# Fusion block: embedded rows kept in a PSUM bank, token mix reading transposed tokens from PSUM, squares in the place of the columns, and another order of work

## The chip, the cores and the metric

One core of one Trainium2 chip. The metric is the device time of one execution in microseconds. The kernel before has a median of 1633.04 us in three runs.

## The reference, cut to what matters

64 pictures of 3x224x224 are cut into 196 patches of 768 numbers; each patch is normalised, multiplied by a 768x256 matrix and normalised again. 77 text tokens are put behind the 196 of the picture, 273 tokens in all. Then comes an attention block, whose attention, by the letters of its einsum, runs over the 16 heads of one token and not over tokens, and a feed-forward block with a token shift, each on normalised rows and added to its input.

```python
x = _layernorm(patches, ln1_g, ln1_b)
x = jnp.einsum('bnd,de->bne', x, W) + b
h = concatenate([_layernorm(x, ln2_g, ln2_b), txt], axis=1)
# attention on _layernorm(h); Q, K, V have the shape (n, heads, tokens, 16)
scores = jnp.einsum('nqhd,nkhd->nhqk', Q, K) * scale
o = jnp.einsum('nhql,nlhd->nqhd', softmax(scores), V).reshape(n, s, e)
h = h + (o @ Wo.T + bo)
# feed-forward on x = _layernorm(h):
x_prev = concatenate([zeros, x[:, :-1, :]], axis=1)
xr = mu_r * x + (1.0 - mu_r) * x_prev
xk = mu_k * x + (1.0 - mu_k) * x_prev
out = sigmoid(xr @ W_r.T) * (square(relu(xk @ W_k.T)) @ W_v.T)
h = h + out
```

## The kernel before, in words

Everything is float32; products are made from a high and a low part of each operand (three matmuls for one). Four pictures form a quad of 4 x 273 = 1092 tokens, cut into three chunks of 364 tokens. A chunk has three row tiles of 126, 126 and 112 rows. There are 16 quads, so 64 pictures and 48 chunks.

A picture passes through these jobs, in the names of the order: `load` (SP, L477: both halves into `xim`), `xcols` (ScalarE, L943: three copies into the column layout `xcols`), `x` (TensorE, L1106: transposes into PSUM), `xh` and `xl` (high and low part into `xT`, L951 on ScalarE, L770 on VectorE), `tok` (TensorE, L1118: two products with 98 patches each), `sq` (ScalarE, L955: squares), `ssq` (VectorE, L765: their sums), `stat`, `statc`, `statr` (sums over patches, L1125, L774, L780), `sqm`, `rstd1` (first scale), `yn` (VectorE, L786: scaled rows into `y`), `st2`, `mv2` (statistics of `y`, L790, L795), `rstd2`, `hg` (VectorE, L800: `y` less its mean times gain, in place), `h` (VectorE, L806: into `yh`), `hdma` (SP: rows into the chunk's tiles).

A chunk passes through: `st3` to `xnl` (normalisation, transpose, parts), `qkv` and `qb` (products and bias, L1026 and L843), `qkv_out`, `qk_in` (L514), `v_in` (through DRAM), `kspread` (ScalarE, L921), `qplace` (VectorE, L829), `s` (scores, L1075), `mx`, `sub`, `exp`, `pt`, `ptc` (L933), `av`, `rec`, `osb` (softmax and values; `osb` is VectorE's L758), `o_out` and `o_in` (through DRAM, nine pieces out and four in; `o_in` of the first two chunks of a quad waits for `o_out` of the chunk behind, one slot of 4000 steps later), `ont` (TensorE, L1152), `onh`, `onl` (L977, L849), `wo`, `h2`, `st4` to `rstd4`, `z`, `zt` (TensorE, L1166: transposed tokens in PSUM), `ztc` (ScalarE, L994: copied to `zT`), `d` (GpSimd, L654: difference of neighbours), `edge` (GpSimd, L660, L661), `mix` (VectorE, L872: four mixes of 128x364), `mixh`, `mixl`, `k`, `kr`, `ksq`, `kah`, `kal`, `r`, `rt`, `val`, `rv`, `add`, `out`.

The order of work is written out by hand in `AT`: each job has a step; a picture job comes again every 3000 steps, a chunk job every 4000, a quad takes 12,000. Every engine issues its jobs in the order of their steps and starts one when the semaphores that it waits for are up. The steps set an order and no times. SP issues all DMAs, in the same order.

`BANK` gives each product or transpose one of the eight PSUM banks. Before TensorE writes into a bank, `turn` makes it wait for the last reader (`READ`) of the job that had the bank before.

The rows that the mix uses are built as `dT` = token less its predecessor (for the first token of a picture the token itself), and `mix` = `dT` * mu + predecessor, where the predecessor is read from `zT` at one column less.

## Time and profile before

| | us |
|---|---|
| median of three runs | 1633.04 |
| lowest, highest | 1625.81, 1639.91 |
| the profiled execution | 1637.46 |
| its span | 1635.7 |

The span is the time from the first to the last instruction of the profiled execution. Busy time is the union of an engine's instructions; a wait is idle time of an engine just before an instruction, put down to what released it last. Matmuls overlap in the pipeline, so TensorE's busy time is not its time at peak. PE is TensorE, DVE VectorE, ACT ScalarE, POOL GpSimd, and SPq the DMA queue of SP.

### The profile page before, as it was taken

The numbers are of one execution on the slowest core, as the hardware profiler recorded it, in microseconds if no ns is written. First come the engines' busy times: TensorE is split into PE (matmuls) and PEld (weight loads), VectorE is DVE, ScalarE is ACT, GpSimd is POOL, SyncE is SP. The second block draws the span as 40 slices with busy tenths as digits, with TensorE's granted clock in tenths as the row PEclk, the third lists the DMA queues.
The fourth block names the chain that finished last, engine by engine and source line by source line (L and its number), as shares of the span: only waits on it lengthen the run. The fifth ranks groups of instructions, "written<-read, shape, count | busy, mean of one in ns | idle before, by whom it ended". The sixth has DMA issues, their size and how long they took to land. (4 is left out here: it accounts for less than half of the span.)

```text
span 1635.7 us, 53680 instructions
## 1 busy us (share of the span) xinstructions
PE 1454.6 (89%) x18762; PEld 1382.2 (85%) x18762; DVE 1332.3 (81%) x3075; ACT 1099.9 (67%) x2230; POOL 973.6 (60%) x1507
## 2 busy tenths in 40 slices
PE   4678899899999999999999999999999999998856
PEld 4677898898998898889898898998988988897756
DVE  5576888798988989898898888898898988888642
ACT  4455777677777776776777676777777776775543
POOL 2121566567656666666766765675675676576556
PEclk8798999999999999999999999999999999999988
DMA  4279979889877887888887896898898799887651
GB/s 121 59 141 138 141 147 150 125 159 157 143 157 141 147 155 143 150 137 165 149 140 157 151 141 127 167 157 141 152 154 140 151 159 140 156 151 118 131 74 37
DMA packets 702658, 227.65 MB, mean 139 GB/s; under 512 B 617470, under 2 KB 673854, under 8 KB 702394
## 3 DMA queue, kind: packets, MB, share of 16 engines
q1 hardware_dynamic: 702394, 224.23, 77.9%
q8 instruction: 153, 2.51, 0.8%
q14 instruction: 111, 0.91, 0.2%
HBM read 121.64 MB, written 89.64 MB: 129 GB/s over the span
## 5 line engine op out<-in xcount | busy, mean ns | idle before, releaser
L1026 PE MATMUL bank<-wqkv,xnT 128*126 128x384 f32 (+1 forms) x1728 | 354.2, 349 | 5.5 <-issue 5.5
L1118 PE MATMUL bank<-wtok,xT 128*98 128x258 f32 x2304 | 310.2, 290 | 12.0 <-DVE xT L770 11.4
L1026 PEld LDWEIGHTS bank<-wqkv,xnT 128*126 128x126 f32 (+1 forms) x1728 | 294.0, 185 | 18.3 <-issue 10.2
L1118 PEld LDWEIGHTS bank<-wtok,xT 128*98 128x98 f32 x2304 | 294.2, 171 | 14.6 <-DVE xT L770 13.2
L667 POOL TENSOR_TENSOR mixp<-mixf,mixp 128x364 fp32r<-128x364 f32 x192 | 185.2, 976 | 107.2 <-ACT mixp L1000 106.6
L921 ACT ACTIVATE arena<-qk,ymask 128x768 f32<-128x768 f32 x192 | 164.0, 926 | 97.6 <-DMA qk<-qkv_dram 97.6
L843 DVE TENSOR_TENSOR qkvt<-bank,bqkv 126x384 f32<-126x384 f32 (+1 forms) x288 | 154.0, 548 | 48.5 <-PE bank L1026 47.0
L654 POOL TENSOR_TENSOR dT<-zT 128x364 f32<-128x364 f32 x96 | 79.7, 851 | 153.9 <-ACT zT L994 153.9
L609 POOL TENSOR_TENSOR rs<-ve,small 126x3 f32<-126x3 f32 (+1 forms) x160 | 150.3, 940 | 12.5
L607 POOL TENSOR_TENSOR ve<-mv,small 126x3 f32<-126x3 f32 (+1 forms) x160 | 58.8, 368 | 158.8 <-DVE mv L865 104.0
L765 DVE TENSOR_REDUCE xs<-xim 84x14 f32<-84x1792 f32 x64 | 128.7, 2011 | 23.1 <-ACT xim L955 22.8
L872 DVE SCALAR_TENSOR_TENSOR mixf<-dT,mus,zT 128x364 f32<-128x364 f32 x192 | 125.8, 676 | 22.4 <-POOL zT L661 19.5
L943 ACT ACTIVATE xcols<-xim 84x640 f32<-84x640 f32 (+1 forms) x192 | 126.1, 693 | 25.4 <-DMA xim<-in_x 24.1
L1026 PE MATMUL bank<-woT,onT 128*126 128x256 f32 (+1 forms) x864 | 121.9, 287 | 12.4 <-DVE onT L849 12.1
L951 ACT ACTIVATE xT<-bank 128x420 fp32r<-128x420 f32 (+1 forms) x192 | 99.9, 532 | 44.5 <-PE bank L1106 44.2
L1026 PE MATMUL bank<-wrT,mixp 128*126 128x256 f32 (+1 forms) x864 | 124.9, 292 | 4.2 <-POOL mixp L667 3.7
L1026 PEld LDWEIGHTS bank<-woT,onT 128*126 128x126 f32 (+1 forms) x864 | 110.6, 186 | 17.7 <-DVE onT L849 16.9
L1026 PE MATMUL bank<-mixp,wkfT 128*128 128x364 f32 x576 | 123.5, 352 | 1.5 <-POOL mixp L667 1.4
L1075 PE MATMUL bank<-arena,qx 128*32 128x64 f32 x4608 | 83.0, 225 | 43.8 <-issue 43.8
L933 ACT ACTIVATE pt<-bank 64x384 f32<-64x384 f32 x192 | 93.0, 484 | 37.9 <-PE bank L1083 34.5
L682 POOL TENSOR_TENSOR h<-h,r 126x256 f32<-126x256 f32 x144 | 114.2, 807 | 6.1 <-DVE r L878 6.1
L1075 PEld LDWEIGHTS bank<-arena,qx 128*32 128x32 f32 x4608 | 74.1, 112 | 51.1 <-issue 47.4
(121 smaller groups left out, 3339.6 us busy)
## 6 DMA issues: line engine op xcount, KB each, us to landing
xim<-in_x SPq DMA_DIRECT2D x128, 294.0 KB
qk<-qkv_dram SPq DMA_DIRECT2D x48, 768.0 KB, 8.3
qkv_dram<-qkvt SPq DMA_DIRECT2D x96, 378.0 KB
arena<-qkv_dram SPq DMA_DIRECT2D x384, 48.0 KB, 3.9
qkv_dram<-qkvt SPq DMA_DIRECT2D x48, 336.0 KB
o_dram<-probs SPq DMA_DIRECT2D x288, 48.0 KB, 1.9
out<-h SPq DMA_DIRECT2D x96, 126.0 KB
on<-o_dram SPq DMA_DIRECT2D x64, 126.0 KB
```

The lines of the kernel that those rows point to most:

```text
L609: done.done(P.tensor_tensor(rs[:, :], ve[:, :], powt[0:part, 0:ve.shape[1]], ALU.pow))
L667: mix_lo.done(P.tensor_tensor(mixp[:, w, 1, kk, :], mixf[:, kk, :], mixp[:, w, 0, kk, :].bitcast(F32), ALU.subtract))
L682: out_sb.done(P.tensor_tensor(dst, dst, r[0:rows, i, :], ALU.add))
L765: x_stats.done(V.tensor_reduce(xs[:, :], xim[:, :].rearrange("p (w q) -> p w q", q=128), AX.X, ALU.add))
L843: qkv_sb.done(V.tensor_tensor(qkvt[0:rows, i, NQ * half:NQ * half + NQ], place("qkv", job)[0:rows, 0:NQ], bqkv[0:rows, :, :].rearrange("p ...
L872: mix_sb.done(V.scalar_tensor_tensor(out=mixf[:, kk, :], in0=dT[:, kk, :], scalar=mus[:, w, kk:kk + 1], in1=zT[:, kk, 0:CT], op0=ALU.mult, ...
L921: kb_sb.done(A.activation(kb[:, :, yy, :], qk[:, :, HD:2 * HD], ACT.Copy, scale=ymask[:, yy:yy + 1]))
L943: x_cols.done(A.activation(xcols[:, 128 * w0:128 * w1].rearrange("p (w r q) -> p w r q", r=HALF, q=PS), xim[:, :].rearrange("p (r w q) -> ...
L951: x_hi.done(A.activation(xT[:, 0, :, w0:w1], src, ACT.Copy))
L1026: ins = mm(psum, left(a, k), right(b, k), start=t == 0, stop=t == len(terms) - 1)
L1075: ins = mm(place("s", part)[32 * j:32 * j + 32, col:col + 64], qx[:, g, :, :].rearrange("p x q -> p (x q)"), kb[:, g, :, :].rearrange("p y ...
L1118: ins = mm(place("tok", c)[0:PT, 0:E + 2], xT[:, a, i0:i0 + GRID // 2, :].rearrange("p i w -> p (i w)"), wtok[:, b, ch, :], start=t == 0, ...
```

## The change

Four things. First, `y` is no tensor in SBUF any more but half a PSUM bank of its own (bank 7): `yn` writes it there, and `st2`, `hg` and `h` read it there; `yn` waits for that bank through `turn`, which VectorE may call now too. The masked statistics `sel`, which lay in `y`, get a small tensor. Second, `mix` reads the transposed tokens in their PSUM bank instead of `zT`. As that is the token itself and not its predecessor, `mus` holds mu - 1, and the memset of the predecessor at picture edges (L661) goes; a bank of `zt` is now given back by `mix` 2 or 3 and no longer by `ztc`. Third, the squares overwrite `xcols` instead of `xim`. So `load` waits for the three copies of the picture before instead of its reduce, `sq` waits for the transposes of its own picture, and the first copy of a picture waits for the reduce of the picture before. Fourth, all steps of `AT` and all banks are new: picture jobs have banks 3 and 1, chunk jobs 0, 2, 4, 5, 6.

```diff
-AT = dict(load=[0], xcols=[1345, 1388, 1607], sq=[2596], ssq=[2858], sqm=[3415, 4248], x=[1817, 2019, 2235],
-    xh=[1848, 2327, 2533], xl=[2074, 2593, 2661], tok=[2893, 3830], stat=[3940], statc=[4050], statr=[4305],
-    rstd1=[4411], txt=[8023], yn=[4758, 4836], st2=[4981, 5034], mv2=[5433, 5999], rstd2=[6371], hg=[6625, 6861],
-    h=[6868, 6960], hdma=[7063], st3=[10962, 11342, 11356], mv3=[11065, 11397, 11434], rstd3=[11873], xn=[12040,
-    12043, 12181], xt=[12258, 12294], xnh=[12466, 12535], xnl=[12759, 12786], hb=[16417], qkv=[13041, 13154, 13772,
-    14109, 14497, 14527], qb=[13342, 13376, 14009, 14120, 14637, 14838], qkv_out=[13386, 14854, 14929],
-    qk_in=[15678], v_in=[16977], qplace=[17149, 17224], kspread=[17070, 17106, 17203, 17246], s=[17531, 17701],
-    mx=[17623, 17710], sub=[17716, 17726], exp=[17794, 17831], pt=[17914, 17953], ptc=[18007, 18037, 18144, 18161],
-    av=[18175, 18232], rec=[18186, 18538], osb=[18451, 18546], o_out=[18883], o_in=[23572], ont=[24528, 24562],
-    onh=[24548, 24569], onl=[24813, 24817], wo=[24929, 25291, 25299], h2=[25035, 25379, 25541], st4=[25320, 25562,
...
+AT = dict(load=[0], xcols=[974, 1452, 2008], sq=[3314], ssq=[3606], sqm=[4006, 4551], x=[2368, 2528, 2871],
+    xh=[2472, 2955, 3124], xl=[2687, 3242, 3261], tok=[3423, 4348], stat=[3670], statc=[4035], statr=[4182],
+    rstd1=[4635], txt=[8796], yn=[5189, 5294], st2=[5527, 5530], mv2=[6117, 6421], rstd2=[7071], hg=[7159, 7405],
+    h=[7476, 7485], hdma=[8110], st3=[11601, 11697, 11879], mv3=[11949, 11981, 12005], rstd3=[12326], xn=[12347,
+    12371, 12403], xt=[12701, 12751], xnh=[12819, 12851], xnl=[13088, 13135], hb=[17111], qkv=[13369, 13634, 14369,
+    14664, 15014, 15279], qb=[13566, 14729, 14730, 14870, 15390, 15419], qkv_out=[15330, 15332, 15987],
+    qk_in=[16906], v_in=[17788], qplace=[17760, 17898], kspread=[17748, 17765, 17780, 17888], s=[18176, 18179],
+    mx=[18317, 18320], sub=[18371, 18448], exp=[18511, 18568], pt=[18545, 18617], ptc=[18591, 18662, 18778, 18835],
+    av=[18778, 18860], rec=[18886, 19014], osb=[18968, 19133], o_out=[19894], o_in=[24612], ont=[24927, 25140],
...
+BANK = dict(x=[3, 1, 3], tok=[3, 1], stat=[1], yn=[7], xt=[2, 6], qkv=[2, 6, 0, 4, 6, 4], s=[5, 4], pt=[5, 2],
+    av=[5, 0], ont=[4, 0], wo=[0, 5, 4], zt=[5, 0], k=[5, 2], r=[6, 2, 6], val=[2, 4, 6])
...
-        READ = dict(x=(x_lo, [1, 2, 3]), tok=(y_sb, [1, 2]), stat=(stat_sel, [1]), xt=(xn_lo, [1, 2]),
+        READ = dict(x=(x_lo, [1, 2, 3]), tok=(y_sb, [1, 2]), yn=(h_sb, [2]), stat=(stat_sel, [1]), xt=(xn_lo, [1, 2]),
-                    ont=(on_lo, [1, 2]), wo=(h2_sb, [1, 2, 3]), zt=(zT_sb, [1, 2]), k=(kr_sb, [1, 2]),
+                    ont=(on_lo, [1, 2]), wo=(h2_sb, [1, 2, 3]), zt=(mix_sb, [3, 4]), k=(kr_sb, [1, 2]),
...
-                            after(x_stats, q, k - 1, 1)
+                            after(x_cols, q, k - 1, 3)
...
+                            P.tensor_scalar(mus[:, :, :], mus[:, :, :], 1.0, None, ALU.subtract).then_inc(probs_clear, 1)
...
-                        edge_sb.done(P.memset(zT[:, :, b], 0.0))
...
-                        x_stats.done(V.tensor_reduce(xs[:, :], xim[:, :].rearrange("p (w q) -> p w q", q=128), AX.X, ALU.add))
+                        x_stats.done(V.tensor_reduce(xs[:, :], xcols[:, :].rearrange("p (w q) -> p w q", q=128), AX.X, ALU.add))
...
-                        h_sb.wait(dve, q, k - 1, 2)
+                        stat_sb.wait(dve, q, k - 1, 1)
...
+                    y = place("yn", 0)[0:PT, 0:2 * E].rearrange("p (c e) -> p c e", c=2)
...
-                            h_sb.wait(dve, q, k - 1, 2)
+                            if c == 0:
+                                turn(dve, q, s, "yn", 0)
...
-                                                               in1=zT[:, kk, 0:CT], op0=ALU.mult, op1=ALU.add))
+                                                               in1=place("zt", kk)[:, 0:CT], op0=ALU.mult, op1=ALU.add))
...
-                                x_tr.wait(act, q, k - 1, 3)
-                                x_sq.wait(act, q, k - 1, 1)
+                                x_stats.wait(act, q, k - 1, 1)
...
+                        x_tr.wait(act, q, k, 3)
                         x_cols.wait(act, q, k, 3)
-                        x_sq.done(A.activation(xim[:, :], xcols[:, :], ACT.Square))
+                        x_sq.done(A.activation(xcols[:, :], xcols[:, :], ACT.Square))
...
-                        mix_sb.wait(act, q, k - 1, 4)
+                        edge_sb.wait(act, q, k - 1, 1)
```

The steps that the text speaks of and that are cut above: `zt` was [26592, 26720] and is [27288, 27294]; `ztc` was [26852, 27151] and is [27372, 27410]; `mix` was [27723, 27748, 28355, 28501] and is [28082, 28139, 28650, 28666]; `mixl` was [28081, 28111, 29157, 30005] and is [28447, 28510, 29976, 30394]; `k` was [28326, 28668] and is [28866, 30101]; `out` was [32565, 33050, 33990] and is [33982, 34383, 35593].

## Rows read from the trace of the kernel before

**Rows 1.** The page: busy us of each engine, share of the span, instructions

```profile
PE 1454.6 (89%) x18762; PEld 1382.2 (85%) x18762; DVE 1332.3 (81%) x3075; ACT 1099.9 (67%) x2230; POOL 973.6 (60%) x1507
```

**Rows 2.** Stretches from:to, us: busy time of each engine, granted clock, DMA share, GB/s

```profile
100.00:1500.00 1400.00, 1298.23 (x17287) 1237.74 (x17286) 1210.23 (x2799) 990.93 (x2011) 867.38 (x1328) 0.99 0.84 147
300.00:1300.00 1000.00, 938.80 (x12434) 896.62 (x12437) 875.73 (x2021) 720.01 (x1469) 646.27 (x981) 0.99 0.84 148
1500.00:1636.00 136.00, 97.25 (x1110) 89.51 (x1108) 63.04 (x146) 65.25 (x141) 81.20 (x114) 0.89 0.50 84
```

**Rows 3.** Timeline of PE, transposes L1152: start, us, what, [idle before <-releaser]

```profile
688.95 0.85 PE L1152 MATMUL bank<-ident,on 126*128 126x126 f32 x6 [0.79 <-DMA on<-o_dram]
...
752.07 0.85 PE L1152 MATMUL bank<-ident,on 126*128 126x126 f32 x6 [1.46 <-DMA on<-o_dram]
...
783.12 0.85 PE L1152 MATMUL bank<-ident,on 126*128 126x126 f32 x6 [1.32 <-DMA on<-o_dram]
```

**Rows 4.** Waits of PE from 300 to 1300 us: total us, times, longest

```profile
PE bank L1075 <- issue: 21.5, 22, 2.9
PE bank L1152 <- DMA on<-o_dram: 20.8, 18, 2.5
PE bank L1026 <- DVE onT L849: 8.5, 13, 0.8
PE bank L1083 <- ACT probs L926: 4.8, 10, 0.5
```

**Rows 5.** Waits of ScalarE from 300 to 1300 us

```profile
ACT probs L926 <- DVE probs L746: 40.6, 22, 4.6
```

**Rows 6.** Groups by line: busy us, mean ns, idle before and releaser

```profile
L765 DVE TENSOR_REDUCE xs<-xim 84x14 f32<-84x1792 f32 x64 | 128.7, 2011 | 23.1 <-ACT xim L955 22.8
...
L872 DVE SCALAR_TENSOR_TENSOR mixf<-dT,mus,zT 128x364 f32<-128x364 f32 x192 | 125.8, 676 | 22.4 <-POOL zT L661 19.5 <-POOL mixp L667 2.9
...
L800 DVE SCALAR_TENSOR_TENSOR y<-y,mv,g2b 98x256 f32<-98x256 f32 x128 | 116.2, 908 | 0.0
...
L806 DVE SCALAR_TENSOR_TENSOR yh<-y,rs,b2b 98x256 f32<-98x256 f32 x128 | 69.9, 586 | 0.0
```

**Rows 7.** Single lines: duration min/median/max ns, first and last start us

```profile
L786 DVE SCALAR_TENSOR_TENSOR y<-bank,rstd,c0b x128: 463/474/485, 35.5 to 1485.5; 98x256 f32<-98x256 f32 x128
...
L800 DVE SCALAR_TENSOR_TENSOR y<-y,mv,g2b x128: 447/476/2754, 41.9 to 1495.3; 98x256 f32<-98x256 f32 x128
...
L806 DVE SCALAR_TENSOR_TENSOR yh<-y,rs,b2b x128: 443/477/1028, 48.7 to 1496.1; 98x256 f32<-98x256 f32 x128
...
L872 DVE SCALAR_TENSOR_TENSOR mixf<-dT,mus,zT x192: 582/593/1215, 178.5 to 1620.4; 128x364 f32<-128x364 f32 x192
```

**Rows 8.** Timeline of VectorE, two runs of L800

```profile
702.82 0.46 DVE L800 SCALAR_TENSOR_TENSOR y<-y,mv,g2b 98x256 f32<-98x256 f32 x1
...
719.38 2.74 DVE L800 SCALAR_TENSOR_TENSOR y<-y,mv,g2b 98x256 f32<-98x256 f32 x1
```

**Rows 9.** Timeline of GpSimd beside these two

```profile
703.45 0.34 POOL L607 TENSOR_TENSOR ve<-mv,small 126x3 f32<-126x3 f32 x1 [2.63 <-DVE mv L865]
...
720.00 1.84 POOL L642 TENSOR_TENSOR hb<-hc,bob 126x768 f32<-126x768 f32 x1
```

**Rows 10.** Timeline of all engines, what VectorE and PE do behind the second

```profile
722.93 0.96 DVE L849 TENSOR_TENSOR onT<-bank,onT 128x364 fp32r<-128x364 f32 x2
...
724.04 0.94 PE L1026 MATMUL bank<-woT,onT 128*126 128x256 f32 x6 [0.70 <-DVE onT L849]
```

**Rows 11.** What waited for two transfers, and time to landing

```profile
  ACT xcols L943: 24.1, 20
...
DMA to landing us min/median/max: 7.2/8.3/10.2
```

**Rows 12.** Timeline of VectorE, last scaling of the attention output of one chunk

```profile
737.61 0.56 DVE L758 TENSOR_TENSOR probs<-bank,mx 128x384 f32<-128x384 f32 x1
```

**Rows 13.** Chain of waits from 1590 to 1636 us, shares by line

```profile
by line: issue 25.0%; POOL mixp L667 15.2%; POOL h L682 13.3%; PE bank L1026 10.1%; ACT on L983 4.9%; POOL dT L672 4.8%; POOL dT L654 3.8%; POOL rs L609 3.8%; POOL kaT L676 2.0%; POOLq L189 1.5%; DVE r L878 0.9%; POOL nm L613 0.9%; POOL ve 
```

More of the change, by code:

```diff
@@ L365, in fusion_kernel, with turn @@
         primed += [(sem, 2 * per) for s in mine if isinstance(s, Own) for sem, per in zip(s.sems, s.pers)]
-        READ = dict(x=(x_lo, [1, 2, 3]), tok=(y_sb, [1, 2]), stat=(stat_sel, [1]), xt=(xn_lo, [1, 2]),
+        READ = dict(x=(x_lo, [1, 2, 3]), tok=(y_sb, [1, 2]), yn=(h_sb, [2]), stat=(stat_sel, [1]), xt=(xn_lo, [1, 2]),
                     qkv=(qkv_sb, [1, 2, 3, 4, 5, 6]), s=(s_sub, [1, 2]), pt=(pt_sb, [2, 4]), av=(o_sb, [1, 2]),
-                    ont=(on_lo, [1, 2]), wo=(h2_sb, [1, 2, 3]), zt=(zT_sb, [1, 2]), k=(kr_sb, [1, 2]),
+                    ont=(on_lo, [1, 2]), wo=(h2_sb, [1, 2, 3]), zt=(mix_sb, [3, 4]), k=(kr_sb, [1, 2]),
                     r=(r_tanh, [1, 2, 3]), val=(rv_sb, [1, 2, 3]))
         JOBS = sorted((AT[kind][j] % PERIOD[kind] + PERIOD[kind] * i, order, kind, j, i - AT[kind][j] // PERIOD[kind])
-                      for order, kind in enumerate(PE_ORDER) for j in range(len(BANK[kind])) for i in range(COUNT[kind]))
-        SPARE = [b for b in range(8) if b not in BANK["x"] + BANK["tok"] + BANK["stat"]]
+                      for order, kind in enumerate(BANK_ORDER) for j in range(len(BANK[kind])) for i in range(COUNT[kind]))
+        SPARE = [b for b in range(8) if b not in BANK["x"] + BANK["tok"] + BANK["stat"] + BANK["yn"]]
         def place(kind, j):
             return banks[BANK[kind][j]]
+        def turn(eng, q, s, kind, j):
+            same = [job for job in JOBS if BANK[job[2]][job[3]] == BANK[kind][j]]
+            at = next(i for i, job in enumerate(same) if job[0] == s and job[2] == kind and job[3] == j)
+            for back in range(1, 8 * len(same)):
+                wrap, i = divmod(at - back, len(same))
+                _, _, other, jj, k = same[i]
+                k += wrap * COUNT[other]
+                if exists(q, k, COUNT[other]):
+                    signal, steps = READ[other]
+                    return signal.wait(eng, q, k, steps[jj])
         SCALE = {0: HD ** -0.5, 6: 0.5}
@@ L1027, in product @@
                 return ins
-            def turn(q, s, kind, j):
-                same = [job for job in JOBS if BANK[job[2]][job[3]] == BANK[kind][j]]
-                at = next(i for i, job in enumerate(same) if job[0] == s and job[2] == kind and job[3] == j)
-                for back in range(1, 8 * len(same)):
-                    wrap, i = divmod(at - back, len(same))
-                    _, _, other, jj, k = same[i]
-                    k += wrap * COUNT[other]
-                    if exists(q, k, COUNT[other]):
-                        signal, steps = READ[other]
-                        return signal.wait(pe, q, k, steps[jj])
             pe.wait_ge(prep_pool, 26)
@@ L1068, in body @@
                                 kb_sb.wait(pe, q, k, 4)
-                            turn(q, s, "s", part)
+                            turn(pe, q, s, "s", part)
                             for b in range(PB * part, PB * part + PB):
@@ L1080, in body @@
                             p_exp.wait(pe, q, k, part + 1)
-                            turn(q, s, "pt", part)
+                            turn(pe, q, s, "pt", part)
                             for row in range(PB // 4):
@@ L1089, in body @@
                                 v_in.wait(pe, q, k, 8)
-                            turn(q, s, "av", part)
+                            turn(pe, q, s, "av", part)
                             for b in range(PB * part, PB * part + PB):
```

48 lines of the change are left out of this document (24 added, 24 removed).

## The prediction

> **What bounds the kernel now.** I first read the busy shares of the page [rows 1]: TensorE 89%, VectorE 81%, the others less. Then the stretches [rows 2]: between 100 and 1500 us TensorE is busy for 1298 of 1400 us at a granted clock of 0.99, VectorE for 1210; the last 136 us hold TensorE for 97 us and VectorE for 63 only. So the kernel is a long steady part, bounded by TensorE with VectorE close behind, with ends bounded by latency. Two reads of the same place of the order, three chunks apart, give the steady pace: 688.95 and 783.12 us [rows 3], 94.2 us for a quad, which the order calls 12,000 steps; one step is 7.85 ns. Below, distances in steps are turned into time with this.
>
> Third, what TensorE waits for in the steady part [rows 4]: of 1000 us it idles 61.2, and the list names 21.5 us before the scores (L1075, "issue": it waits for spread keys and placed queries, both of which stand behind the DMA that brings q and k back), 20.8 before the transposes of the attention output (a DMA from DRAM), 8.5 for VectorE's low part of the attention output (L849), 4.8 for the exponentials, which themselves wait 40.6 us for VectorE's subtraction [rows 5]. 61 us in 1000 is all that a change which leaves the matmuls alone can win: over 1400 us, 86 us. More than that can't come.
>
> **Part 1: three operations leave SBUF.** The diff puts the embedded rows `y` into a PSUM bank and lets the token mix read the transposed tokens where TensorE left them. The operations that change are L800, L806 and L872. Their means are 908, 586 and 676 ns [rows 6]. The same form with one operand in PSUM, L786 (98x256 too), has a median of 474 and lies between 463 and 485 ns in all 128 of its runs [rows 7]. L800 lies between 447 and 2754 ns with a median of 476 [rows 7]. So not the work but something beside it costs: at 702.82 us, with GpSimd idle for the 2.63 us up to 703.45, L800 takes 0.46 us; at 719.38 it takes 2.74, across the whole of a GpSimd sum of 1.84 us that starts at 720.00 [rows 8, 9]. Both inputs of L800 and L806 are in SBUF, as are those of L872; L786, with one input in PSUM, never shows it. The Trainium skill says so outright (SBUF — State Buffer, "SBUF: two separate sides"): a VectorE instruction with two SBUF inputs and a GpSimd instruction lock each other out for a whole instruction. The rows agree: L800 ends after the sum does.
>
> Worth in busy time: L800 116.2 us less 128 x 0.474 = 60.7 gives 55.5; L806 69.9 less 60.7 gives 9.2; L872 125.8 less 192 x its own median of 0.593 = 113.9 gives 11.9. Sum 76 us of VectorE's 1332 [rows 1]. GpSimd is locked out less in its turn, which I leave uncounted, as the memset L661 that goes.
>
> No VectorE row writes to PSUM, and none takes bn_stats from there. Reading: L786 with a PSUM source has a median of 474 ns, L806, the same size from SBUF alone, 477 [rows 7]. So a PSUM source costs nothing here, and I price it at zero; as bounds for reading and writing I take 50 ns less or more on each of the 256 writes (yn, hg), 13 us of VectorE either way. Against this stands a rule: the Trainium skill (VectorE: DVE Perf Modes, "The TRN2 errata") gives 120 cycles of fixed cost with a PSUM source and 58 with SBUF at 0.96 GHz, 65 ns more each; for the 576 instructions that now read PSUM (bn_stats, hg, h, mix) that estimate is 37 us of VectorE given back. The 3 ns between L786 and L806, of the other sign, speak against it.
>
> How much of 76 us reaches TensorE? A direct case is in [rows 8, 10]: L800's 2.74 us stands in VectorE's queue ahead of L849, and TensorE then idles 0.70 us before the output projection at 724.04, released by L849. I give the change all of that wait (8.5 us per 1000), half of the exponentials' (2.4), and half of the scores' (10.7; the bias adds ahead of it come sooner, and the order leaves 2757 steps instead of 2693 between the last bias add and the scores, 0.5 us more). Sum 21.6 per 1000 us, times 1.4 = **-30 us**. Bounds: -12 (L849's wait alone) and -60 (70% of all idle time).
>
> **Part 2: the picture path.** The squares go into `xcols`, so the load L477 waits only for the copies (L943). The copies of the next picture now wait for the reduce L765: it stands at step 3606 and takes 2.01 us [rows 6] = 256 steps, so it ends at 3862, and the next copies stand at 3974: 0.9 us of slack. If VectorE is later than that, ScalarE stands still, with the PSUM copies L951 and L933 and the exponentials L926 behind it, and TensorE behind those. The squares wait for the transposes, 443 steps (3.5 us) ahead of them: covered. The load loses lead: 1345 steps to its copies before, 974 now (10.6 and 7.6 us), but it no longer waits for the reduce, which ended at 3114, 114 steps into the next image, so 9.7 us stood against 7.6. ScalarE already waits 24.1 us for it in total [rows 11], and will wait longer; the transposes stand 1394 steps behind the first copy (10.9 us; before 472), so TensorE doesn't see it. Price 0, bounds -3 and +15. The wait of L774 for `yh` of the picture before is gone, that of the row scaling for its bank is the old one under another name: 0.
>
> **Part 3: banks.** `y` owns bank 7; the picture's transposes, products and statistics share banks 3 and 1 instead of 5, 7 and 2; all chunk work has five banks instead of six. A transposed-token bank used to be free 320 or 491 steps after its start (2.5 to 3.9 us); it is now held until mix 2 or 3 has ended, 1437 or 1447 steps (11.3 us). The first user after it is K's product at 28866 in bank 5: mix 2 starts at 28650 and takes 0.59 us = 75 steps, so 141 steps, 1.1 us, remain. K must wait for the low part of the mix anyway (28510 + 125 steps). Price 0, bounds 0 and +20.
>
> **Part 4: the new order.** From VectorE's last attention scaling (L758, of the chunk behind, so a slot later than its own step) to the transposes of the attention output lay 18546 + 4000 to 24528, 1982 steps; now 19133 + 4000 to 24927, 1794: 14.1 us instead of 15.6, start to start. Between them SP must send nine pieces to DRAM, wait, and fetch four. In the trace one such trip took from 737.61 to 752.07, 14.5 us, and TensorE waited 1.46 us at its end [rows 3, 12]. With 1.5 us less, such a chunk waits up to 1.5 us more; 18 waits in the 32 chunks of 1000 us [rows 4] say that more than half are such. VectorE, being less late, takes most of that back: I take 0.3 us on ten of the 48 chunks, **+3**, bounds -10 and +72 (1.5 us on all 48). Second, the last output stands at step 35593 instead of 33990, so a chunk is in flight 1603 steps longer, 12.6 us at the steady pace. In the last stretch only dependences count (the chain of waits there runs through GpSimd's mix and ScalarE's normalisation [rows 13], and they are the same), so I take less than half, **+5**, bounds 0 and +12.6. The one tensor_scalar on `mus` runs once at the start: 0.
>
> **Sum.** The profiled execution took 1637.5 us (span 1635.7 and 1.8 around it). 1637.5 - 30 + 0 + 0 + 3 + 5 = 1615.5; it lies 4.4 above the median of the runs, so 1611; I say **1610**.
>
> **The rivals.**
> A: relief off the path. VectorE idled 124 us in 1000 already, and 42 of the 61 us of TensorE's idle time name DMA round trips, which no VectorE operation shortens. Then only L849's wait goes: -12 + 8 gives 1629. For it: DMA is busy 84% [rows 2], and the q and k transfer takes 8.3 us to land [rows 11]. Against: the round trips start when VectorE has finished.
> B, slower: the transposes of the attention output wait for the fetch. TensorE is in order, so K, the projections and the pictures queue behind it. At 1.5 us on all 48 chunks it costs 72, less 30, plus 5: 1680. It decides from 0.5 us per chunk (24 us, which eats the relief); at 0.9 it is slower than now by 1%. For it: the wait is the second largest today and the room shrinks by 10%. Against: 14 of 32 chunks didn't wait at all [rows 4].
> C: the change doesn't do what it says, since PSUM operands carry a price. By the bound of 50 ns on 256 writes VectorE keeps 63 of 76 us; even at 0.1 us on all 832 touched instructions (83 us), it is just back at today's load, and with the +8 of part 4 the time is 1641.
>
> **How the numbers follow.** Forecast 0.50 (1580 to 1617), A 0.24, C 0.05, B 0.21. A measurement of this kernel can tell about 1% from no change; 1% is 1616.7 and 1649.4. Faster is 0.48 of the forecast case and 0.02 of A; same is 0.02 of the forecast, 0.22 of A, 0.05 of C and 0.03 of B; the other 0.18 of B is slower. The range reaches from 1578 (the bound of -60, with the -3 of the picture path) to 1655 (B at 1 us per chunk, beside a relief of 25).
>
> **What would show it.** The L800 and L806 successors at 0.47 us with no long ones, mix at 0.59, VectorE's busy time near 1256; TensorE's wait for L849 near zero. Wrong would be: the wait before the transposes of the attention output above 50 us in total (B), the reduce-to-copy wait showing on ScalarE with TensorE's waits behind it, or statistics from PSUM over 0.46 us (C).

## The result, and the profile after

The changed kernel takes 1683.97 us (median of four runs, 1665.23 to 1688.16); the kernel before took 1634.47 us in the runs beside it. The ratio is **1.029**, with a 95% interval from 1.0195 to 1.0376: slower, where 1610 us was forecast. The profiled execution, the longest of the four, has a span of 1686.4 us, against 1635.7 before. First the page: busy us of each engine, share of the span, instructions [rows 1].

```profile
PE 1475.3 (87%) x18762; PEld 1402.3 (83%) x18762; DVE 1289.2 (76%) x3075; ACT 1116.1 (66%) x2230; POOL 894.0 (53%) x1460
```

The span grew by 50.7 us. TensorE's busy time grew by 20.7 (from 1454.6, with the same 18762 matmuls) and its idle time by 30.0 (from 181.1 to 211.1). VectorE's fell by 43. Next the stretches [rows 2]: length, busy time of PE, PEld, DVE, ACT and POOL, granted clock, DMA share, GB/s.

```profile
100.00:1500.00 1400.00, 1274.22 (x16738) 1217.38 (x16739) 1134.05 (x2711) 978.06 (x1949) 767.59 (x1239) 0.96 0.83 143
300.00:1300.00 1000.00, 912.42 (x11892) 872.53 (x11881) 810.44 (x1941) 701.40 (x1410) 566.71 (x913) 0.97 0.83 143
```

The loss lies in the steady part, where a quad now takes 97.0 us instead of 93.9 (mean of twelve): of 1000 us TensorE idles 87.6 instead of 61.2, its granted clock is 0.97 instead of 0.99, and it gets through 11892 matmuls instead of 12434. What it waits for there [rows 4]: total us, times, longest.

```profile
PE bank L1157 <- DMA on<-o_dram: 36.4, 18, 4.6
PE bank L1080 <- ACT arena L938: 26.1, 11, 4.1
PE bank L1080 <- DVE qx L844: 7.7, 11, 1.2
PE bank L1080 <- issue: 6.3, 3, 4.0
PE bank L1088 <- ACT probs L943: 3.1, 8, 0.5
```

Read this against the list of before. The wait for the low part of the attention output is gone (8.5). The wait before the transposes of the attention output (L1157, was L1152) rose from 20.8 to 36.4. The wait before the scores (L1080, was L1075), which had stood as "issue" with 21.5, now has three names, 26.1 + 7.7 + 6.3 = 40.1. Two waits for trips through DRAM grew by 15.6 and 18.6 us, 34.2 together; 8.5 + 1.7 went. In all 11 waits that name ScalarE's spreading of the keys (L938), the first of its four copies starts 0.02 to 0.03 us after q and k have landed, and the four follow each other without a pause; so ScalarE isn't late there, the transfer is. The groups of VectorE that the change touches, and one that it doesn't [rows 6]: busy us, mean ns, idle before.

```profile
L889 DVE SCALAR_TENSOR_TENSOR mixf<-dT,mus,bank 128x364 f32<-128x364 f32 x192 | 106.3, 586 | 29.6 <-POOL dT L673 28.4 <-POOL mixp L679 1.0 <-issue 0.3
L844 DVE COPY qx<-qk 64x768 f32<-64x768 f32 x96 | 102.8, 1071 | 45.1 <-DMA qk<-qkv_dram 43.5
L815 DVE SCALAR_TENSOR_TENSOR bank<-bank,mv,g2b 98x256 f32<-98x256 f32 x128 | 61.8, 483 | 0.0
L821 DVE SCALAR_TENSOR_TENSOR yh<-bank,rs,b2b 98x256 f32<-98x256 f32 x128 | 55.4, 475 | 0.0
```

`hg` fell from a mean of 908 to 483 ns, `h` from 586 to 475, `mix` from 676 to 586. The placing of the queries (L844, SBUF to SBUF, which the diff leaves as it is) rose from 630 to 1071 ns. The longest of its runs, with GpSimd beside it, from the timeline of all engines:

```profile
457.60 2.55 DVE L844 COPY qx<-qk 64x768 f32<-64x768 f32 x1
458.24 0.74 POOL L694 TENSOR_TENSOR h<-h,r 112x256 f32<-112x256 f32 x1
458.94 0.80 POOL L684 TENSOR_TENSOR dT<-dT 128x364 f32<-128x364 f32 x1
459.69 1.29 POOL L679 TENSOR_TENSOR mixp<-mixf,mixp 128x364 fp32r<-128x364 f32 x1
```

Of the 96 placings of queries 31 take under 600 ns, and GpSimd does nothing in any of these; in the 32 that take over 1000 it works for 1.76 us on average. Before, 77 were short and 11 long.

Then one trip of the attention output, from the timeline of all engines: start, us, engine, line, tile [rows 3, 12].

```profile
731.23 0.56 DVE L770 TENSOR_TENSOR probs<-bank,mx 128x384 f32<-128x384 f32 x1
...
732.35 4.36 SPq L540 DMA_DIRECT2D o_dram<-probs  x9
...
736.83 0.34 SPq L519 DMA_DIRECT2D qkv_dram<-qkvt  x1
...
737.29 0.91 SPq L488 DMA_DIRECT2D xim<-in_x  x2
...
738.53 1.44 SPq L550 DMA_DIRECT2D on<-o_dram  x4
...
745.80 1.48 PE L1157 MATMUL bank<-ident,on 126*128 126x126 f32 x6 [2.33 <-DMA on<-o_dram]
```

The last scaling ends at 731.79, the nine writes go out, then a write of q, k and v, both halves of a picture load, and the fetch; the transposes start 14.0 us behind the scaling. Without the 2.33 us of waiting TensorE would have come to them after 11.7 us. In the same way the trip of before [rows 3, 12] took 13.9 us from the end of the scaling, of which TensorE waited 1.46: there it came after 12.4.

I made this count for 36 chunks of either trace. In each kernel just one chunk of three has a picture load between its writes and its fetch, as here. Those took 14.1 us before and 14.65 after; TensorE waited 1.27 us in each before, and 3.0 after. The chunks whose fetch follows directly took 11.2 us before, without a wait, and 12.6 after, also without one (there TensorE itself came no sooner). The third kind fetches a whole slot after its writes; its wait is 0.72 us before and 0.67 after. So the whole growth of this wait falls on the chunks with a load inside.

**The clock.** The granted clock behind the longer waits, in short stretches of the changed kernel (columns as above): the wait of 3.06 us that ends at 843.00, and what follows.

```profile
840.00:843.00 3.00, 0.00 (x0) 0.00 (x1) 0.61 (x3) 0.79 (x2) 1.96 (x2) 1.00 1.29 210
844.30:847.70 3.40, 3.40 (x18) 3.40 (x17) 1.93 (x5) 2.03 (x6) 0.20 (x1) 0.53 1.17 113
848.00:856.00 8.00, 7.68 (x141) 7.31 (x140) 7.18 (x14) 5.37 (x9) 5.14 (x6) 1.00 0.66 82
```

TensorE does nothing for 3 us; about 1.5 us after it has begun again the granted clock falls to the lower level, 1.2 GHz, while it is busy throughout the stretch shown, and then it is back at 2.4. The trace of before shows the same behind a wait of 2.46 us that ends at 939.76:

```profile
936.00:939.60 3.60, 1.31 (x9) 1.00 (x7) 1.48 (x4) 1.44 (x3) 3.44 (x5) 1.00 1.16 208
939.60:943.00 3.40, 3.24 (x18) 3.16 (x19) 2.96 (x7) 2.75 (x7) 2.15 (x4) 0.65 1.57 142
```

By my count of the clock records, stretches at the lower level add up to 171.6 us after and 106.6 before; between 300 and 1300 us to 58.0 in 14 stretches instead of 19.4 in 5. Of the 20 waits of TensorE of 2 us or more between 150 and 1500 us of the changed kernel, 17 have such a stretch beginning in them or within 4 us of their end. 65 us more at half the clock are up to 32 us of work lost, against the 20.7 by which TensorE's busy time grew. No experiment holds the clock fixed, so that these 20.7 us are the clock's is an inference from this count.

### The profile page after: what moved, and what is told of

It is laid out like the page before. It is cut to its first block and busy times, and to the rows that moved or that the text cites. A ratio compares the mean times of both kernels' runs of the same rounds, so it can differ in the third digit from the quotient of the medians.

```text
span 1686.4 us, 53698 instructions
## 1 busy us (share of the span) xinstructions
PE 1475.3 (87%) x18762; PEld 1402.3 (83%) x18762; DVE 1289.2 (76%) x3075; ACT 1116.1 (66%) x2230; POOL 894.0 (53%) x1460
## 5 line engine op out<-in xcount | busy, mean ns | idle before, releaser
L1123 PE MATMUL bank<-wtok,xT 128*98 128x258 f32 x2304 | 328.1, 300 | 10.4 <-DVE xT L782 6.0
L1123 PEld LDWEIGHTS bank<-wtok,xT 128*98 128x98 f32 x2304 | 306.6, 178 | 14.9 <-DVE xT L782 7.0
L938 ACT ACTIVATE arena<-qk,ymask 128x768 f32<-128x768 f32 x192 | 164.0, 925 | 90.1 <-DMA qk<-qkv_dram 90.1
L858 DVE TENSOR_TENSOR qkvt<-bank,bqkv 126x384 f32<-126x384 f32 (+1 forms) x288 | 154.2, 548 | 73.2 <-PE bank L1043 71.2
L959 ACT ACTIVATE xcols<-xim 84x640 f32<-84x640 f32 (+1 forms) x192 | 132.9, 695 | 46.4 <-DMA xim<-in_x 35.8
L1080 PEld LDWEIGHTS bank<-arena,qx 128*32 128x32 f32 x4608 | 82.4, 119 | 77.7 <-issue 60.6
L1080 PE MATMUL bank<-arena,qx 128*32 128x64 f32 x4608 | 90.8, 238 | 64.2 <-ACT arena L938 40.5
L684 POOL TENSOR_TENSOR dT<-dT 128x364 f32<-128x364 f32 x96 | 76.4, 795 | 120.8 <-ACT dT L1022 120.8
L777 DVE TENSOR_REDUCE xs<-xcols 84x14 f32<-84x1792 f32 x64 | 128.3, 2004 | 14.4 <-ACT xcols L972 13.9
L844 DVE COPY qx<-qk 64x768 f32<-64x768 f32 x96 | 102.8, 1071 | 45.1 <-DMA qk<-qkv_dram 43.5
L620 POOL TENSOR_TENSOR rs<-ve,small 126x3 f32<-126x3 f32 (+1 forms) x160 | 127.2, 795 | 12.5
L632 POOL TENSOR_TENSOR var<-stat,mean 98x2 f32<-98x2 f32 x64 | 12.6, 196 | 222.9 <-issue 194.7
L889 DVE SCALAR_TENSOR_TENSOR mixf<-dT,mus,bank 128x364 f32<-128x364 f32 x192 | 106.3, 586 | 29.6 <-POOL dT L673 28.4
L618 POOL TENSOR_TENSOR ve<-mv,small 126x3 f32<-126x3 f32 (+1 forms) x160 | 31.1, 194 | 182.5 <-DVE mv L880 132.3
L1111 PE MATMUL bank<-ident,xcols 84*128 84x84 f32 x896 | 100.4, 246 | 24.1 <-DVE bank L801 17.6
```

The costliest lines, as they stand in the source:

```text
L620: done.done(P.tensor_tensor(rs[:, :], ve[:, :], powt[0:part, 0:ve.shape[1]], ALU.pow))
L777: x_stats.done(V.tensor_reduce(xs[:, :], xcols[:, :].rearrange("p (w q) -> p w q", q=128), AX.X, ALU.add))
L844: q_sb.done(V.tensor_copy(qx[half, :, xx, :], qk[half, :, 0:HD]))
L858: qkv_sb.done(V.tensor_tensor(qkvt[0:rows, i, NQ * half:NQ * half + NQ], place("qkv", job)[0:rows, 0:NQ], bqkv[0:rows, :, :].rearrange("p ...
L889: mix_sb.done(V.scalar_tensor_tensor(out=mixf[:, kk, :], in0=dT[:, kk, :], scalar=mus[:, w, kk:kk + 1], in1=place("zt", kk)[:, 0:CT], op0= ...
L938: kb_sb.done(A.activation(kb[:, :, yy, :], qk[:, :, HD:2 * HD], ACT.Copy, scale=ymask[:, yy:yy + 1]))
```

## The experiments

Eighteen kernels, each set against the kernel before on the same chip. In x2, x3, x9 to x12 and x16 the banks were assigned anew by the distance between last read and next write; x12 shows what one such assignment does, and x10 below what another does.

**The new order and its parts.** x1: the new `AT` and `BANK`, but `y` in SBUF, the mix from `zT`, squares into `xim`.

```diff
+AT, BANK of the changed kernel; everything else as before
```

> The steps and banks of the changed kernel, with all operands where they were: y in SBUF, the mix reading zT, the squares in xim (only the small tensor sel of its own, which the new order needs). Theory O, the new order costs and the moved operands give: at least as slow as the changed kernel, ratio to before 1.03 to 1.05, with TensorE's waits before the scores and before the attention output's transposes as large as in the changed kernel, and L800's like back at a mean of 0.8 us or more. Theory M, the moves to PSUM and the squares in the columns' place cost: within 1% of before.

Measured: 1861.46 us, ratio 1.139 [1.131, 1.147]. The longest wait of TensorE in 1000 us:

```profile
PE bank L1211 <- DMA on<-o_dram: 66.8, 18, 6.0
```

and of SP:

```profile
SPq L343 <- DVE xs L824: 219.9, 37, 10.8
```

Neither theory had this size. The order can't be run without the moves: the fetch wait is nearly twice that of the changed kernel. With squares in `xim` the load must wait for the reduce (step 3606, 606 steps into the next picture's 3000); SP stands at it for 219.9 of 1000 us, and everything behind it in the queue leaves late. Which of the three moves mends how much wasn't tried but for `y` (next). `hg` has a mean of 721 ns here, with `y` in SBUF, against 908 before: the new order alone takes away a part of its stretching.

x8: the changed kernel with `y` back in SBUF.

```diff
+        y = sb("y", [PT, 2, E])
-                    y = place("yn", 0)[0:PT, 0:2 * E].rearrange("p (c e) -> p c e", c=2)
```

> The changed kernel, with y back in SBUF (and bank 7 unused). The value of y in PSUM inside the new order: VectorE is busy for about 65 us more through hg and h, at 0.8 us or more a piece. If this relief carries into the time, the ratio to before is 1.05 or more; if the waits of TensorE for the DMAs cover it, it is 1.03 like the changed kernel.

Measured: 1684.55 us, 1.0287 [1.0225, 1.0349], the time of the changed kernel, though VectorE is busy 1329.4 us instead of 1289.2. Its waits:

```profile
PE bank L1213 <- DMA on<-o_dram: 36.1, 19, 3.7
PE bank L1136 <- ACT arena L982: 25.0, 9, 4.2
PE bank L1136 <- DVE qx L888: 7.4, 11, 1.1
PE bank L1136 <- issue: 6.2, 5, 2.3
```

The same list within 1.1 us; TensorE idles 84.3 us in 1000, against 87.6 with `y` in PSUM. In the new order 40 us of VectorE's time are worth nothing that can be measured; the two intervals leave room for about 1% either way. `hg` takes 92.2 us here and 61.8 in the changed kernel, `h` 72.5 and 55.4.

**The moves in the old order.** x2: `y` in a PSUM bank; x3: mix from PSUM; x4: squares in the columns' place, the old banks; x16: both of these.

```diff
 # x2, the old steps
+            yn=[5], and y = place("yn", 0)..., with turn(dve, q, s, "yn", 0) ahead of yn
 # x3, the old steps
-                in1=zT[:, kk, 0:CT]
+                in1=place("zt", kk)[:, 0:CT]
 # x4
-  x_sq.done(A.activation(xim[:, :], xcols[:, :], ACT.Square))
+  x_sq.done(A.activation(xcols[:, :], xcols[:, :], ACT.Square))
```

> The old steps, only y in a PSUM bank of its own, and the other jobs spread anew over the seven banks left, so that by the steps one pair of jobs overlaps by 109 steps (0.85 us), four times a quad. Theory O: the mean of the subtraction of hg falls to 0.48 us, VectorE's busy time by about 64 us, ratio 0.98 to 1.00. Theory M: slower than before, 1.01 or more.

Measured: 1705.72 us, 1.043 [1.037, 1.049].

```profile
PE bank L1166 <- DVE bank L858: 24.2, 20, 1.8
PE bank L1098 <- DVE bank L858: 21.6, 10, 2.9
```

L858 is `yn`. It is the last reader of the bank of `tok`, and with a bank fewer for the rest, a transpose of the next picture (L1166) stands right in front of its end, and a product of K (L1098) waits for it too. VectorE's busy time fell to 1286.3 us, about as far as in the changed kernel. The bank that `y` takes, as the banks are assigned here, costs more than the relief gives.

> The old steps, only the mix reading the transposed tokens in PSUM, all eight banks assigned anew since a bank of transposed tokens is held four times as long. Theory O: mix at 0.59 us, VectorE's busy time 12 us less, ratio 0.99 to 1.005. Theory M, the long hold of these banks makes TensorE wait: 1.01 or more, with waits of TensorE on the mix in the list.

Measured: 1643.99 us, 1.0048 [1.0015, 1.0081]. VectorE's busy time fell to 1311.1, and TensorE waits 29.0 us in 1000 for `yn`, by the banks again.

> The old steps and the old banks, only the squares written over the columns, so that the load waits for the copies only and the next copies wait for the reduce. Both theories O and M leave this open; if the earlier load helps, ScalarE's wait for the picture falls from 24 us and the ratio is 0.99 to 1.00; if the chain copies, squares, reduce, copies is what costs, it is above 1.01.

Measured: 1633.72 us, 1.0003 [0.9959, 1.0048]. Part 2 of the prediction, priced at zero, is zero in the old order.

> Old steps, the mix from PSUM and the squares in the columns' place, with banks assigned anew so that the reuse of a bank stands 100 steps behind its last reader where that is possible (in x3 TensorE waited 29 us in 1000 for y before the picture's transposes, from reuse with no distance). If the relief of the mix counts once the banks don't bind: 0.99 to 1.00. If a bank held for four times as long costs what the relief gives: 1.00 to 1.01.

Measured: 1634.92 us, 0.9985 [0.9953, 1.0018]. Both moves together, in the old order with a better assignment of banks, change nothing that can be measured.

x12: the old kernel with another assignment of banks and nothing else.

> The kernel before with nothing but the banks assigned anew, by the rule used in x9 to x11: no two jobs of a bank overlap by the steps. It is the measure for these three. If only overlaps of holds count, the ratio is within 0.5% of 1; if the assignment itself matters, since a bank's last reader is often late, it is up to 1.02.

Measured: 1638.3 us, 0.9991 [0.9962, 1.0020]. This assignment is neutral.

**Room.** All steps from `ont` to `out` moved by 150 (with `hb`), so that the transposes of the attention output come 1.2 us later or sooner.

```diff
 # x9: changed kernel; x11: kernel before
+    every step of ont, onh, ... out, and hb: + 150
 # x10: kernel before
+    the same: - 150
```

> The changed kernel, with all chunk jobs from the attention output's transposes to the store 150 steps later (1.2 us), the fetch where it was, and the banks assigned anew for it (one pair of jobs overlaps by 84 steps). Theory R, the order leaves these transposes too little room behind the last scaling: the wait there falls from 36 us in 1000 to under 15, and the ratio to before from 1.029 to 1.01 or less, since fewer long waits also mean less time at the lower granted clock. Rival S, the time is set by a chain that runs through both trips to DRAM and back, so that a wait taken away at one comes back at the other: the wait before the scores grows by what the first one loses, ratio 1.02 to 1.04.

Measured: 1799.07 us, 1.0996 [1.0936, 1.1056].

```profile
PE bank L1100 <- POOL mixp L736: 38.9, 26, 3.1
PE bank L1137 <- DVE h L929: 16.5, 22, 2.5
...
PE bank L1214 <- DMA on<-o_dram: 8.5, 7, 1.9
```

The wait that was to shrink did, from 36.4 to 8.5, and yet the kernel is ten per cent slower than before: GpSimd's mix comes in late for K's product, and the scores wait for VectorE's `h2` (L929), which reads a bank that they get.

> The kernel before, with the same jobs 150 steps earlier (1.2 us) and the banks assigned anew. Theory R: the wait before the transposes rises from 20.8 us in 1000 to over 35, ratio 1.015 to 1.03, which is most of what the change lost. Rival S: within 1% of x12.

Measured: 1794.43 us, 1.0945 [1.0891, 1.1]. TensorE doesn't wait for the fetch; it waits 56.1 us for ScalarE's `dT` and 29.3 for `on`. The 56.1 us stand before the output projection, which doesn't use `dT`: `dT` is what `kr` makes, the last reader of K's bank, and the new assignment gives that bank to the projection next. So this run tests the banks more than the room.

> The kernel before, with the same jobs 150 steps later and the banks assigned anew. Theory R: the wait falls from 20.8 us in 1000 to under 8, ratio 0.985 to 0.995. Rival S: within 1% of x12, or slower.

Measured: 1740.38 us, 1.0632 [1.0576, 1.0689], with 38.7 us of waiting for `on`. These three say nothing about the two trips: a block moved as a whole upsets its neighbours, and the banks moved with it, so the two effects aren't separated. As tests of the room they failed.

**What stands in SP's queue.** x5: in the changed kernel the picture load moved from step 0 to -380, which takes it from between writes and fetch. x6: the values' fetch waits until q and k have landed. x7: both.

```diff
 # x5
-AT = dict(load=[0], ...
+AT = dict(load=[-380], ...
 # x6, ahead of v_in
+                        after(qk_in, q, k, 1)
```

> The changed kernel, with the step of the picture load at -380 instead of 0, so that it stands at least 992 steps ahead of the fetch of the attention output instead of 612. Theory Q, the picture load in the DMA queue right in front of that fetch makes TensorE wait: the wait before the transposes of the attention output falls from 36 us in 1000 to under 15, ratio to before 1.00 to 1.015. Theory R, the room in the order between the last scaling and these transposes is too small whatever stands in the queue: that wait stays above 25 us, ratio 1.02 to 1.03.

Measured: 1731.81 us, 1.0577 [1.0497, 1.0657].

```profile
PE bank L1080 <- ACT arena L938: 56.2, 13, 6.2
PE bank L1157 <- DMA on<-o_dram: 15.3, 17, 2.6
...
PE bank L1080 <- issue: 12.5, 7, 3.9
...
PE bank L1080 <- DVE qx L844: 4.8, 4, 1.4
```

The trip of the attention output in the chunks that had a load inside fell from 14.65 to 12.4 us, and TensorE's wait for it from 36.4 to 15.3. The wait before the scores rose from 40.1 to 73.5: in every third chunk the load now stands between the fetch of the attention output and that of q and k, which there takes 10.4 us to land instead of 8.1. The load's place decides which trip is late.

> The changed kernel, with the fetch of the values made to wait until q and k have landed. Theory Q, what is queued on the DMA engines beside a fetch is what makes TensorE wait: q and k land in less than 7.8 us, the wait before the scores falls from 40 us in 1000 to under 20, ratio 1.00 to 1.015. Theory R: q and k land as before, the values come later, and the wait moves to the products with the values; ratio 1.03 or more.

Measured: 1686.75 us, 1.0295 [1.0221, 1.0369], fetch wait 38.2, before the scores 34.2. Q and k landed after 8.3 us on average instead of 8.65, and SP stood 114.7 us in 1000 at the new wait. Taking the values' fetch from beside that of q and k wins nothing in this queue; what it would do without SP's standing isn't shown.

> Both of these edits. Theory Q: the two waits together fall from 76 us in 1000 to under 35, ratio 0.98 to 1.005. Theory R: 1.02 or more.

Measured: 1737.13 us, 1.0624 [1.0543, 1.0706], near x5; the two waits are 26.7 and 61.1 us.

**Less to transfer.** x13 (the old order with x4's squares) and x14 (the changed kernel) leave out most of the picture load: after the first picture, only 256 of 1792 columns of each half are loaded, so the rest of `xim` is stale. Everything else is computed as before. x15 is x14 with `y` in SBUF.

```diff
+                            n = HALF * SIDE if q * IPQ + k == 0 else 256
-                            x_in.done(sp.dma_start(xim[half * 42:half * 42 + 42, :],
+                            x_in.done(sp.dma_start(xim[half * 42:half * 42 + 42, 0:n],
```

> Old steps and banks with the squares in the columns' place (x4, which was equal to before), and from the second picture on only 256 of 1792 columns of each half of a picture are loaded; the rest of xim keeps old data, so what is computed for these pictures is not the reference. It takes 32 MB of some 228 off the DMA engines and leaves every instruction of the compute engines. It is the measure for x14 and x15. Theory T, the trips of q, k, v and of the attention output through loaded DMA engines hold TensorE up: ratio to before 0.975 to 0.99. Rival U, the chip's time here is set by how the engines' own queues interleave, and the waits for DMAs only show it: 0.99 to 1.00.

> The changed kernel with the same small loads. Theory T: the waits before the scores and before the attention output's transposes fall from 76 us in 1000 to under 30, few stretches at the lower clock are left, and the ratio to before falls from 1.029 to 0.98 to 0.995, at or below x13. Rival U: 1.015 to 1.03.

Measured: x13 1601.07 us, 0.9796 [0.9762, 0.9830]; x14 1619.16 us, 0.9917 [0.9886, 0.9948]. The waits of x14:

```profile
PE bank L1081 <- ACT arena L939: 21.8, 10, 2.9
PE bank L1081 <- issue: 13.9, 8, 2.2
PE bank L1158 <- DMA on<-o_dram: 10.3, 14, 1.7
PE bank L1081 <- DVE qx L845: 4.4, 4, 1.2
```

and of x13:

```profile
PE bank L1076 <- issue: 12.3, 11, 2.0
...
PE bank L1153 <- DMA on<-o_dram: 6.6, 11, 1.4
```

The same relief of the DMA engines gives the old order 2.0% and the new one 3.6%, and new over old falls from 1.029 to 0.9917 / 0.9796 = 1.012. In x14 the trip with a load inside takes 11.8 us instead of 14.65, and TensorE waits 0.2 us for it instead of 3.0. What is left is the wait before the scores, 21.8 + 13.9 + 4.4 = 40.1, as large as with the whole loads.

> x14 with y back in SBUF. Where TensorE no longer waits for the trips, the 40 us that VectorE saves through y may count: slower than x14 by 1 to 2% if they do, equal within 0.5% if VectorE is off the path in this order whatever the DMAs do.

Measured: 1618.16 us, 0.9913 [0.9873, 0.9953], x14's time. Even with the transfers cut VectorE's relief shows nothing in this order; the intervals leave about 0.5% either way.

**The queue, tried from the other side.** x17: in the changed kernel the writes of the attention output go out right behind the last scaling and ahead of the writes of q, k and v. x18: x4 with the load right behind the fetches.

```diff
 # x17
-    osb=[18968, 19133], o_out=[19894],
+    osb=[18968, 19133], o_out=[19140],
 # x18
-AT = dict(load=[0], ...
+AT = dict(load=[-300], ...
```

> The changed kernel, with the nine writes of the attention output (o_out) at step 19140, right behind the last scaling (19133) and ahead of the writes of q, k and v (15330, 3330 in its slot), instead of at 19894, behind two of them. By the theory that SP stands still before those writes (it waits 44.7 us in 1000 for VectorE's bias adds) and holds the attention output back: in the chunks whose fetch follows in the same slot, the first write leaves 1.7 us after the last scaling and should leave at 0.2; TensorE's wait for the fetch falls from 36.4 to about 20 us per 1000, the time to about 1655, ratio 1.01 to 1.015. By the theory that the writes and the fetch are slow because the picture load stands between them in the queue: the wait stays above 30 and the time at 1.025 to 1.03. If the nine writes now delay q and k, the wait before the scores grows beyond 40.1 by what the other wait loses.

Measured: 1790.59 us, 1.099 [1.087, 1.112]. What SP waits for in 1000 us:

```profile
SPq L283 <- DVE probs L770: 126.4, 29, 11.0
```

and TensorE:

```profile
PE bank L1157 <- DMA on<-o_dram: 66.8, 19, 5.3
```

The writes left 0.16 us after the scaling, as they should, and the theory fell all the same. SP now stands at them for 126 us, everything behind them leaves late, and the three writes of q, k and v, held up meanwhile, come between writes and fetch: the fetch is issued 5.2 us after the last write, where it was 2.2, and the trip with a load inside takes 16.5 us instead of 14.65.

> The kernel before with the squares in the columns' place (ratio 1.000) and the picture load at step -300 instead of 0: it then stands right behind the fetch of q and k of every third chunk (3678 in its slot, load 3700) and no load stands between the writes of the attention output (2883) and its fetch (3572), where one stood in every third chunk. In the kernel before, just those chunks take 14.1 us from the last scaling to the transposes and the others 11.2. By the theory that this load in the queue makes the wait: TensorE's wait for the fetch falls from 19.6 to below 10 us per 1000, and the time by up to 1%, unless the load now slows the landing of q and k, which shows as a longer wait before the scores (14.2). By the rival that the load's place means nothing: both waits as they are, ratio 1.00.

Measured: 1634.28 us, 1.0028 [0.9989, 1.0067].

```profile
PE bank L1075 <- issue: 27.6, 24, 3.0
PE bank L1152 <- DMA on<-o_dram: 15.0, 16, 1.6
```

Against x4 the wait for the attention output fell from 19.6 to 15.0 and the wait before the scores rose from 14.2 to 27.6. The trip that had the load inside took 13.3 us instead of 14.1. As in x5, one wait fell and the other rose by more, 8.8 us in 1000 together, here without a measurable change of the time.

No version that computes the whole result beat both kernels; x4, x12, x16 and x18 equal the kernel before. Two of the moves cost nothing in the old order (x4, x16) and the third gives and costs nothing in the new one (x8), and the changed kernel's list has next to no wait for a bank. What is left as the cause of the 2.9% is the order of the steps.

## Why the prediction was wrong

**The step that failed** is "How much of 76 us reaches TensorE?", taken at -30. For the relief through `y` it is zero within the noise: the changed kernel and x8 take the same time, and so do x14 and x15. The relief of the mix was measured in the old order only, with x16, and is nothing there too. The premise was partly right. The wait behind a stretched `hg` did vanish (8.5 in 1000 us), as the direct case in [rows 10] said, and the exponentials' wait fell from 4.8 to 3.1. But in the new order the first of them is gone with `y` in SBUF too (x8's list). And the largest credit, half the wait before the scores (-10.7), had the wrong sign: that wait rose by 18.6. It rested on 2757 steps instead of 2693 between the last bias add and the scores. In the traces TensorE, where nothing holds it, comes to the scores 17.8 us after the end of the last bias add, and before it was 18.5: the room is 0.7 us smaller, not 0.5 larger. And the chain inside it is longer. On average of 36 chunks the last write of q, k and v leaves 3.5 us after the add instead of 2.9 and the fetch 8.1 us instead of 7.3. This last write stands behind the nine of the attention output, in both kernels, and these now leave later themselves. SP stands more at the writes of q, k and v ahead of them, which is the likely reason, not tried alone: what SP waits for in 1000 us was before

```profile
SPq L284 <- DVE qkvt L843: 11.1, 15, 1.9
```

and is now

```profile
SPq L283 <- DVE qkvt L858: 44.7, 39, 4.1
```

Steps give an order and no times; I had said so of the kernel and then turned a difference of 64 steps into a gain.

**Part 1, the work itself**, was right in all three operations: [rows 6] fell by 54.4, 14.5 and 19.5 us, 88 where 76 was forecast. By x8, 24.0 of the 54.4 come with the new order, which leaves `hg` less often beside GpSimd, and 30.4 with the move. (Rival C's 832 touched instructions count the 128 of `hg` twice, as reader and as writer; there are 704.) VectorE's busy time came to 1289 and not 1256, as the placing of the queries took 42 us more. It took between 537 and 1205 ns, and takes 540 to 2546 now: it reads and writes SBUF, and GpSimd's work now lies beside it. The Trainium skill's rule of the lock (SBUF — State Buffer, "SBUF: two separate sides") names this case beside that of two SBUF inputs: a VectorE operation in a two-port mode, which a float32 copy from SBUF to SBUF triggers. The trace agrees, with the 31 short and 32 long copies above; I had applied the rule to what the diff touches, and not to what the new order moves next to GpSimd. The other rule, that a PSUM source costs 65 ns more for each instruction (VectorE: DVE Perf Modes, "The TRN2 errata"), doesn't show here: `hg` has a median of 483 ns, writing to PSUM as well, `h` 475 against 477, and the statistics 417 against 411.

**Part 2** at 0: right (x4). In the changed kernel ScalarE waits 35.8 us for the picture instead of 24.1 and 9.4 for the reduce, the sign that was named; but between 300 and 1300 us no wait of TensorE names the picture's copies, and where TensorE waits for ScalarE's keys, ScalarE itself had waited for the transfer. **Part 3**, banks at 0 with a bound of 20: between 300 and 1300 us the changed kernel's list has 0.3 us of waiting for a bank (the picture's transposes for `yn`), so right there; 17.2 us more stand in the first 190 us, where it was 6.1 before, and the first 100 us still hold as much work (59.3 us busy, 59.2 before). x2 shows that zero is no property of the move: with the banks of x2, the old order with `y` in a bank is 4.3% slower.

**Part 4**, +3 with a bound of +72, is the other step that failed, by size. The mechanism is rival B's. The +3 came to 15.6 us in 1000, 22 over 1400: the room is 0.7 us less in the trip shown and 1.2 us less on average of the chunks with a load inside (11.65 instead of 12.8), where "1.5 us less" stood, and VectorE didn't take it back, since the trip starts when SP gets to the writes: in these chunks 1.7 us after the last scaling instead of 0.65. The wait grew by 1.7 us on each chunk of one kind out of three. B had 1.5 us on all 48 chunks and its price of 1680 came close, but by luck, since its faults cancel: only a third of the chunks pay for that trip (22 us, not 72), the relief of 30 that it subtracts isn't there, and it left out the other trip, that of q and k (26 us), and the clock. My own bound said that B decides from 0.5 us per chunk; 1.7 on a third is 0.57. The wait before the transposes "above 50 us in total", named as the sign of B, was just met: 52.2 over the whole run, against 29.0 before. The +5 for the end isn't there: from the last chunk's first transposes of the attention output to the end it is 31.5 us, against 32.3 before.

**What no case had** is the clock. Of the 50.7 us, 30.0 are idle time and 20.7 are more busy time for the same matmuls, with more of it at the lower clock. I counted every wait once. The split is that of one execution: x8, 2.1 us shorter in span, has 37.9 us of idle time and 10.7 of busy time more than before, at a clock of 0.958 instead of 0.949.

**The sum as measured**: relief 0, the two trips +34 in 1000 us or +48 over 1400, less what the order takes away of other waits (-10 in 1000, -14), gives +34 of idle time. The trace has 24.0 more between 100 and 1500 us and 30.0 over the whole run; with 20.7 for the clock the sum is 55 against 50.7.

**What stays open.** Of the 2.9%, some 1.7 go when the picture loads are small (x13, x14): with them the wait for the attention output falls by 26 us in 1000 in the new order and by 13 in the old (x4 to x13), and the time at the lower clock between 300 and 1300 us from 58.0 to 20.5 us. The remaining 1.2% stand beside a wait before the scores of 40.1 against 12.3. For that, the smaller room and the later writes of q, k and v are read from the trace, the slower placing of the queries as well, though TensorE's waits name it for 7.7 us in 1000 only; none of the three was tried alone, and x17 shows that this queue can't be changed at one place.

## What to carry to other kernels

Relief on the second busiest engine counts only as far as the bounding engine waits for it in the order that will run, so price it there. In a kernel with one in-order queue for all transfers, look at each trip through DRAM for what the new order puts between its writes and its fetch, and at the queue's own waits; distances in a hand-written order are no times. And a long wait of TensorE can cost more than its length: here 17 of the 20 waits of 2 us or more went with a stretch at the lower clock.

## What was not expected of the hardware

- Behind its longer waits, as the 3.06 us before 843.0, TensorE's granted clock fell to 1.2 GHz after it had begun again: 58.0 us in 14 stretches between 300 and 1300 us, 19.4 in 5 before. Over the whole run the granted clock was 0.949, against 0.968 before, and 0.926 in x1 and x17.
- VectorE writes to a PSUM bank nearly as fast as to SBUF: `yn` has a median of 483 ns against 474, `hg` 483 against 476, in all 128 runs of `hg` between 473 and 489.
- A copy of 64x768 from SBUF to SBUF on VectorE takes from 540 ns, without GpSimd, to 2546 beside it.
- One DMA issue mostly held SP for 0.3 to 0.5 us. The eight fetches of the values held it for 4.3 us at 781.26, and for 12.8 us at 740.84, right behind a load and two fetches.
